# Graph attention with a residual LayerNorm on one core: the last three tiles in an order of their own on each engine, and the closing rounds' preparation inside their branch

## The reference

```
h  = x @ W
s1 = h @ attn[:256, 0];  s2 = h @ attn[256:, 0]
e  = leaky_relu(s1[:, None] + s2[None, :], 0.2)
e  = where(adj > 0, e, -9e15)
h2 = elu(softmax(e, axis=1) @ h)
out = layernorm(x + h2)          # over the last axis, eps 1e-5, no scale or shift
```

## Time and profile before

| what | value |
|---|---|
| median of 3 runs | 861.21 us (860.45 to 862.23) |
| profiled execution, device time | 860.82 us |
| its span | 859.1 us |
| mean granted TensorE clock | 0.883 |
| busy: PE, DVE, ACT, POOL | 70%, 72%, 67%, 71% of the span |
| DMA queues | 0.82 of 16 engines for the `adj` stream and the other SP transfers, 0.105 for the gathers |

### The profile page before, as it was taken

One profiled execution on the slowest core, in us unless ns is written; L12 is line 12 of the kernel. 1 busy time (PEld: TensorE's weight loads), 2 busy tenths in 40 slices (PEclk: granted clock), 3 DMA queues, 4 the chain that ended last, 5 costly groups with the idle time before them and its releaser, 6 DMA issues.

```text
span 859.1 us, 10648 instructions
## 1 busy us (share of the span) xinstructions
PE 598.4 (70%) x2590; PEld 385.8 (45%) x2633; DVE 614.6 (72%) x2385; ACT 577.6 (67%) x531; POOL 607.0 (71%) x695
## 2 busy tenths in 40 slices
PE   5588986646858777586787675777648775786641
PEld 4466662424536445353454343544425353454331
DVE  4257552567688987779897587788858877887863
ACT  3034536668777987878787497686959858897510
POOL 4487425778778777587865888888888786887742
PEclk9799999788978999898898988889889897999966
DMA  8999997999999999999999999999999998999400
GB/s 324 401 399 408 388 382 313 411 419 407 416 376 412 416 418 415 416 418 411 404 398 420 415 382 406 374 362 372 417 402 405 408 416 340 396 416 419 154 23 31
DMA packets 62850, 320.21 MB, mean 373 GB/s; under 512 B 19286, under 2 KB 37943, under 8 KB 46400
## 3 DMA queue, kind: packets, MB, share of 16 engines
q1 hardware_dynamic: 36176, 285.49, 81.7%
q0 software_dynamic: 25456, 29.79, 10.5%
q10 hardware_dynamic: 1152, 4.19, 1.2%
HBM read 344.79 MB, written 17.14 MB: 421 GB/s over the span
## 4 chain that ended last, share of the span: by engine, by line
issue 24%; POOL 20%; DMA 20%; DVE 17%; PE 15%; ACT 2%; POOLq 1%; SPq 0%; ACTq 0%; DVEq 0%
POOL GATH L1474 18%; DMA GATH<-haug,ids 7%; DMA ADJ<-in_adj_dram 6%; PE acc L513 6%; DMA WORK<-in_adj_dram,smalls 3%; DMA X<-in_x_dram 3%; PE pk L527 3%; PE acc L538 3%; DVE GATH L761 2%; ACT WORK L1296 2%; DVE diag L834 2%; PE mid_acc L604 1%; DVE smalls L775 1%; DVE WORK L951 1%; DVE PART L844 1%
## 5 line engine op out<-in xcount | busy, mean ns | idle before, releaser
L1474 POOL DMA_INDIRECT GATH<-haug,ids x448 | 471.5, 1053 | 132.5 <-issue 128.7
L1296 ACT ACTIVATE WORK<-ADJ 128x4096 bf16<-128x4096 int32 x128 | 461.9, 3609 | 138.7 <-PE pk L527 83.5
L527 PE MATMUL pk<-WORK,D 128*128 128x512 bf16 x981 | 256.6, 411 | 129.8 <-ACT WORK L1296 125.9
L527 PEld LDWEIGHTS pk<-WORK,D 128*128 128x128 bf16 x1024 | 100.1, 103 | 264.3 <-ACT WORK L1296 150.2
L538 PE MATMUL acc<-GATH,diag 128*128 128x256 f32 x512 | 157.3, 462 | 80.6 <-DVE diag L834 80.6
L538 PEld LDWEIGHTS acc<-GATH,diag 128*128 128x128 f32 x512 | 117.2, 235 | 123.6 <-DVE diag L834 99.2
L513 PE MATMUL acc<-Waug,GATH 128*128 128x258 f32 x256 | 64.8, 396 | 12.5 <-DVE GATH L761 12.5
L844 DVE SCALAR_TENSOR_TENSOR PART<-GATH,smalls,PART 128x256 f32<-128x256 f32 x128 | 62.2, 486 | 4.5
L770 DVE MAX8 smalls<-pk 128x8 f32<-128x512 f32 x64 | 44.5, 695 | 28.5 <-issue 28.2
L513 PEld LDWEIGHTS acc<-Waug,GATH 128*128 128x128 f32 x256 | 48.3, 196 | 24.9 <-issue 17.3
L604 PE MATMUL mid_acc<-X,WORK 128*128 128x256 f32 x256 | 58.0, 380 | 0.0
(11 more groups left out here) (180 smaller groups left out, 775.7 us busy)
## 6 DMA issues: line engine op xcount, KB each, us to landing
ADJ<-in_adj_dram SPq DMA_DIRECT2D x128, 2048.0 KB, 15.1
haug<-GATH POOLq DMA_DIRECT2D x32, 258.0 KB, 9.0
out_dram<-Y SPq DMA_DIRECT2D x32, 256.0 KB
GATH<-haug,ids POOLq DMA_INDIRECT x448
X<-in_x_dram SPq DMA_DIRECT2D x1, 4096.0 KB, 33.8
WORK<-in_adj_dram ACTq DMA_DIRECT2D x8, 512.0 KB
X<-in_x_dram SPq DMA_DIRECT2D x1, 3072.0 KB, 26.8
X<-in_x_dram SPq DMA_DIRECT2D x1, 1024.0 KB, 7.1
```

Of the source, the lines that this page charges most:

```text
L527: done = nc.tensor.matmul(pk[s % PKS][:], D16[:, k, :], A16[:, q % 2, k * BW:(k + 1) * BW], start=(half == 0 and k == 0), stop=(half == 1 ...
L1296: act.activation(A16[:, q % 2, :], ADJ[:, q % 4, :], ACT.Relu, scale=HALF_SCALE if q % 2 else 1.0, accum_out=degree[:, q // 2, q % 2:q % 2 ...
L1474: pool.indirect_dma_start(out=GATH[:, r, k * DA:(k + 1) * DA], out_offset=None, in_=haug, in_offset=bass.IndirectOffsetOnAxis(ap=ids[:, t ...
```

## The change

The loops over steps `T` to `LAST` are taken out of every engine's program, and the last three tiles' stations are written out by hand, for each engine in its own order. The heavy rows are counted by one product of their own on PE, right after DVE's sums, into a free part of `list_ps`; DVE copies the count into `n_heavy` in passing. The ranks, the constants and the load of `s2` move into the branch of the closing rounds, and the register load with the one branch that is left goes to the end of every engine's program.

```diff
+        heavy_total = sem("heavy_total")
+        heavy_counted = sem("heavy_counted")
         def heavy_rows(eng):
-            eng.wait_ge(rank_steps, 2)
+            eng.wait_ge(heavy_counted, 1)
             return eng.value_load(n_heavy[0:1, 0:1], min_val=0, max_val=N)
...
             pe.wait_ge(heavy_noted, 2)
-            pe.wait_ge(mid_list_steps, 1)
-            nc.tensor.transpose(list_ps[0:T, 0:P], heavy[:], ident[:]).then_inc(turned, 1)
...
-            n = heavy_rows(pe)
-            with pe.If(n > 0):
+            nc.tensor.matmul(list_ps[0:1, 3 * P:3 * P + 1], ones, heavy_in_row, start=True, stop=True)\
+                .then_inc(heavy_total, 1)
+            mid_project(1)
+            for t in range(T - 3, T):
+                slots(t)
+
+            def rank_rows():
+                pe.wait_ge(mid_list_steps, 1)
+                nc.tensor.transpose(list_ps[0:T, 0:P], heavy[:], ident[:]).then_inc(turned, 1)
...
-            for s in range(T, LAST + 1):
-                for t in softs_at(s - 1):
-                    slots(t)
-                mid_pieces(s)
...
-            rounds(pe, n, None, dense_round)
+            rounds(pe, heavy_rows(pe), rank_rows, dense_round)
...
             dve.tensor_reduce(heavy_in_row, heavy[:], AX_X, ALU.add).then_inc(heavy_noted, 1)
-            dve.wait_ge(turned, 1)
-            dve.tensor_copy(heavyT, list_ps[0:T, 0:P]).then_inc(turned_copied, 1)
-            dve.wait_ge(ranks_ready, 1)
-            dve.scalar_tensor_tensor(out=rank, ...).then_inc(rank_steps, 1)
-            dve.tensor_copy(n_heavy[0:1, :], pk[1][0:1, 0:1]).then_inc(rank_steps, 1)
-            dve.wait_ge(rank_steps, 1)
-            dve.tensor_scalar(rank, rank, -1.0, None, ALU.add).then_inc(rank_ready, 1)
-            after_scan(T - 1)
+            soft_logits(T - 3)
+            mid_copy_agg(1)
+            dve.wait_ge(heavy_total, 1)
+            dve.tensor_copy(n_heavy[0:1, :], list_ps[0:1, 3 * P:3 * P + 1]).then_inc(heavy_counted, 1)
+            residual(G - 3)
+            soft_weights(T - 3)
+            mid_copy_h(1)
+            soft_logits(T - 2)
+            soft_weights(T - 2)
+            aggregate(G - 2)
+            mid_residual(1)
+            normalise(G - 3)
+            soft_logits(T - 1)
+            soft_weights(T - 1)
+            residual(G - 2)
+            aggregate(G - 1)
+            mid_normalise(1)
+            normalise(G - 2)
+            residual(G - 1)
+            normalise(G - 1)
...
-            for s in range(EARLY, LAST + 1):
-                if s < T:
-                    count(2 * s)
+            for s in range(EARLY, T):
+                count(2 * s)
...
+            soft_exp(T - 3)
+            mid_elu_exp(1)
+            soft_exp(T - 2)
+            elu_exp(G - 2)
+            soft_exp(T - 1)
+            elu_exp(G - 1)
...
             for t in range(T):
-                if t == T - 1:
-                    dense_constants()
                 gather(t)
...
-            n = heavy_rows(pool)
-            with pool.If(n > 0):
-                prepare(0)
...
+            mid_inverse_std(1)
+            inverse_std(G - 2)
+            mid_store(1)
+            inverse_std(G - 1)
...
-            def load_s2():
+            def first():
+                dense_constants()
                 pool.wait_ge(mid_stored, 32)
                 pool.dma_start(s2_all, s2_row...).then_inc(s2_loaded, 16)
-
-            rounds(pool, n, load_s2, dense_round)
+                prepare(0)
+
+            rounds(pool, heavy_rows(pool), first, dense_round)
```

More of the change, by code:

```diff
@@ L676, in _ @@
             pe.wait_ge(heavy_noted, 2)
-            pe.wait_ge(mid_list_steps, 1)
-            nc.tensor.transpose(list_ps[0:T, 0:P], heavy[:], ident[:]).then_inc(turned, 1)
[L679 to L685, removed]
-            n = heavy_rows(pe)
-            with pe.If(n > 0):
+            nc.tensor.matmul(list_ps[0:1, 3 * P:3 * P + 1], ones, heavy_in_row, start=True, stop=True)\
[6 more added lines that the diff above has]
+                nc.tensor.transpose(list_ps[0:T, 0:P], heavy[:], ident[:]).then_inc(turned, 1)
+                pe.wait_ge(dense_consts, 7)
+                pe.wait_ge(turned_copied, 1)
+                nc.tensor.matmul(list_ps[:, P:P + T], heavyT, before[0:T, 0:T], start=True, stop=False)
+                nc.tensor.matmul(list_ps[:, P:P + T], before, heavy_in_row.broadcast_to([P, T]),
+                                 start=False, stop=True).then_inc(ranks_ready, 1)
                 list_rows(0, 0)
                 list_rows(0, 1)
-            for s in range(T, LAST + 1):
-                for t in softs_at(s - 1):
-                    slots(t)
-                mid_pieces(s)
             def dense_round(g, more):
@@ L1141, in _, with rank_rows @@
             dve.tensor_reduce(heavy_in_row, heavy[:], AX_X, ALU.add).then_inc(heavy_noted, 1)
-            dve.wait_ge(turned, 1)
-            dve.tensor_copy(heavyT, list_ps[0:T, 0:P]).then_inc(turned_copied, 1)
-            dve.wait_ge(ranks_ready, 1)
-            dve.scalar_tensor_tensor(out=rank, in0=list_ps[:, P:P + T], scalar=1.0, in1=heavy[:], op0=ALU.add,
-                                     op1=ALU.mult).then_inc(rank_steps, 1)
-            dve.tensor_copy(n_heavy[0:1, :], pk[1][0:1, 0:1]).then_inc(rank_steps, 1)
-            dve.wait_ge(rank_steps, 1)
-            dve.tensor_scalar(rank, rank, -1.0, None, ALU.add).then_inc(rank_ready, 1)
-            after_scan(T - 1)
+            soft_logits(T - 3)
[18 more added lines that the diff above has]
+            normalise(G - 1)
+            def rank_rows():
+                dve.wait_ge(turned, 1)
+                dve.tensor_copy(heavyT, list_ps[0:T, 0:P]).then_inc(turned_copied, 1)
+                dve.wait_ge(ranks_ready, 1)
+                dve.scalar_tensor_tensor(out=rank, in0=list_ps[:, P:P + T], scalar=1.0, in1=heavy[:], op0=ALU.add,
+                                         op1=ALU.mult).then_inc(rank_steps, 1)
+                dve.wait_ge(rank_steps, 1)
+                dve.tensor_scalar(rank, rank, -1.0, None, ALU.add).then_inc(rank_ready, 1)
             L = 4 + CH
@@ L1269, in dense_round @@
                 dve.bn_aggr(mean_var[:, 0, 0, :], stats[:, 0, :]).then_inc(dense_steps, 1)
-            n = heavy_rows(dve)
-            with dve.If(n > 0):
+            dve.wait_ge(agg_ready, G)
+            dve.memset(gate[:, 4:5], 0.0).then_inc(sum_taken, 1)
+            def first():
+                rank_rows()
                 mark_ranks(0, 0)
@@ L1275, in _ @@
                 finish_list(0)
[L1276 to L1279, removed]
                 dve.wait_ge(s2_loaded, 16)
@@ L1283, in _ @@
                 make_logits(0, [0])
-            dve.wait_ge(agg_ready, G)
-            dve.memset(gate[:, 4:5], 0.0).then_inc(sum_taken, 1)
-            rounds(dve, n, lambda: make_logits(0, [1]), dense_round)
+                make_logits(0, [1])
+            rounds(dve, heavy_rows(dve), first, dense_round)
         @block.scalar
@@ L1374, in _ @@
                 count(q)
-            for s in range(EARLY, LAST + 1):
-                if s < T:
-                    count(2 * s)
+            for s in range(EARLY, T):
+                count(2 * s)
                 for x in chunk_at(s - 2):
                     mid_penalise(x)
-                if s < T:
-                    count(2 * s + 1)
+                count(2 * s + 1)
                 for t in softs_at(s - 1):
```

## The result

The new kernel takes 852.33 us (median of 4 runs, 851.30 to 854.12) against 860.83 before: a ratio of 0.9904, 95% interval 0.9886 to 0.9923, which is 8.3 us less, between 6.6 and 9.8 (the medians differ by 8.5). The forecast was 852.7, in a range of 850.5 to 856.0.

A forecast was written before the change was run, and what follows sets the result against it. DVE's program order and the waits in it bound the tail: last normalise at 841.5, + 2.60 + 0.75 + 5.76 = 850.6, a span 8.5 us shorter. Off the 861.21 median that gives 852.7 us, range 850.5 to 856.0.

The forecast's parts named there:

- Sum to last `normalise`: DVE's tail from the heavy rows' last sum to the end of normalise(31): about 25.3 us in place of 34.5.
- exposed softmax: DVE waits for ACT between logits and weights of tiles 62 and 63: 1.35 us in place of 0.78, twice.
- forecast wait of 0.14 for PE at `aggregate(31)`: DVE's wait for slots(63) on PE shrinks from 2.46 us to 0.14, with slots(63) taking 3.73 us.
- Heavy block: DVE between heavy rows' sum and soft_logits(61): transpose, constants, ranks and count took 3.79 us; 3.65 of waits go.
- The two waits for PE: DVE's aggregate(30) waiting 1.75 us for slots(61) and aggregate(31) 2.46 us for slots(63); 1.75 and 2.3 go.
- Store ahead of the last `inverse_std`: On POOL, mid_store(1) stood ahead of inverse_std(31), making normalise(31) wait; 2.2 us go.
- Register load at the end: POOL's register load now follows the gate waiting for the stores: 0.75 us added, bounds 0 and 1.0.
- Gathers: POOL's gathers of tile 63 land at 827.6, ahead of soft_logits(63) at 829.2: slack 1.6 us.
- POOL's closing branch: Rival: POOL's taken branch at the end brings in code, adding 0.4 to 3.7 us: 853.1 to 856.4; chance 0.13.
- all seven more: Rival: tile 63's seven gathers, slowed beside DVE, land too late for soft_logits(63): 853.3 or 855.9; chance 0.11.
- the case in which nothing is gained: Rival: POOL's drain grows by what the tail loses, so the time stays at 860 to 861; chance 0.04.
- its mirror case: POOL's drain shrinks by some 2 us because its last indirect DMA lies further back: 850.5; chance 0.05.

The follow-up runs named there:

- the softmax's wait filled: New kernel with mid_copy_h(1) and normalise(29) each put between a tile's soft_logits and soft_weights, and ACT's soft_exp(62) ahead of mid_elu_exp(1): 851.90 us, ratio 0.9886.
- the last sum at once: New kernel with aggregate(31) moved directly behind soft_weights(63), ahead of residual(30): 855.31 us, ratio 0.9924 to the kernel before.

## Why the prediction was right

The time was forecast at 852.7 and came at 852.33. The tail was to fall by 8.5 us and fell by 9.07. That the times agree within 0.4 us is in part luck, as the four runs lie 2.8 us apart; what bears the forecast out is the steps:

- *Sum to last `normalise`*: forecast 25.3 us, measured 24.73 (818.49 to 843.22). An exposed softmax was put at 1.35 and took 1.33 (824.64 to 825.97) and 1.28 (831.04 to 832.32). A forecast wait of 0.14 for PE at `aggregate(31)` did not come in this execution: `slots(63)` took 2.76 us, not 3.73, at a granted clock that averaged 0.70 from 833.4 to 836.4 us, between its two levels, where I had taken the lower one. With the ranks back and in the kernel in which POOL does not wait, the clock there was 0.50, `slots(63)` took 3.78, and the wait was 0.16. In its place `normalise(30)` waited 0.18 for POOL here. `soft_logits(61)` overlaps the end of the sum, which gave 0.1 more; the rest is steps that came a little shorter than their prices.
- *Heavy block*: shown by putting it back: 4.07 us with the new order, 3.94 of them between the sum and the first logits (3.86 in place of an overlap of 0.08). I had 3.65.
- *The two waits for PE*: gone, and one came back in full when its step was moved (2.57 us).
- *Store ahead of the last `inverse_std`*: 2.2 forecast, 2.25 measured when it was put back.
- *Register load at the end*: 0.75 forecast, 0.78 measured by moving it.
- *Gathers*: the landing never held DVE. It came closest with the softmax's wait filled, where `soft_logits(63)` starts 1.64 us after the end of the last gather (827.17 to 828.81) and does not wait. The forecast had that end 10.0 us behind the sum; with the constants in the branch it lay at 8.5 in five kernels and at 9.9 to 10.3 in three. What the gathers did hold is POOL's `inverse_std(29)` behind them, which only the old order felt.

The rivals: POOL's closing branch took 50 ns, so no code fetch showed on it. The Trainium skill's page "Runtime: NRT & Kernel Launch", section "Instruction fetch mechanics", has a taken branch wait for a fetch when its target is not among the pages on chip. That rule has no case on this engine; where the target lay, no run shows. Beside the denser DVE work one gather of tile 63 took 1.07 us (820.74) and the other six 0.99 to 1.03, never all seven more. POOL's store took 1.60 beside DVE's steps, but 1.06 in the kernel with the last sum at once, where it also lies beside them (840.11); what makes it longer the runs do not show, and nothing waited for it. The drain kept its length, so the case in which nothing is gained and its mirror case both fall.

What the forecast did not see: without the new order, taking the preparation out is worth less than its own waits add up to (1.96 us, where 3.4 was expected), because POOL's order becomes the bound. And it took the wait for the stores at the end as given; that was the largest piece still to be had.

## What to carry to other kernels

In a tail where no engine is full, lay out the one engine whose program order sets the end, and put between the producer and the consumer of every hand-over a step that has to be done anyway; each such swap was worth 0.4 to 3.4 us here. Work for a case that may not occur belongs behind its branch, and the register load that decides it in a place where its engine waits for something else. Look at what each engine waits for after its last useful operation: a wait that another engine makes anyway kept POOL's drain of 5.3 us behind the last store.

## What the runs showed of the hardware

- POOL's drain at the end of the program took 5.30 to 5.385 us in eight profiles, whether its last indirect DMA lay 4.5 or 7.2 us back; where POOL ended early, 1.4 us behind that DMA, it was listed with 5.9, of which about 5.3 lie behind the last operation. What it does in that time the runs do not show.
- PE's closing branch takes 3.3 to 3.9 us in all ten profiles, 3.774 in the new kernel, where it ends 1.9 us after the last matmul. In the kernel before the two end together, in the other eight it ends 0.5 to 1.7 us later. So it is not the wait for `slots(63)` alone, as I had held possible, and what it is stays open; on POOL, ACT and DVE the closing branch took 0.05 to 0.08. PE has no work left behind it, so it costs nothing here.
- The point where the tail begins scatters by 2.8 us between executions of the same work, more than several of the effects told here. Tails measured from one event of the program are finer than whole times: in three kernels with the same steps on DVE (the new one, the load early, POOL not waiting) the stretch from the sum's end to the end of the last `normalise` took 24.73, 24.74 and 24.92 us. Each kernel has one profile, so this is all that shows how finely they resolve.
